# The second routing pass of the first expert network: eight short pieces before the gating of rows 8 to 15, instead of four after the gating of rows 9 to 12

## The reference, cut to what matters

```
def _route(x, gate_weight, expert_bias):
    logits = x @ gate_weight.T                  # 16 experts
    scores = jax.nn.sigmoid(logits)
    biased = scores + expert_bias[None, :]
    ... # the best 2 of 4 groups of 4, by the sum of their two best
    ... # the best 4 experts of the groups kept
    w = jnp.take_along_axis(scores, sel, axis=1)
    w = w / (w.sum(-1, keepdims=True) + 1e-20)
    return (w * SCALING, sel)

def _moe(x, w, sel, gate_proj, up_proj, down_proj):
    cw = (jax.nn.one_hot(sel, NUM_EXPERTS, dtype=x.dtype) * w[..., None]).sum(1)
    def body(acc, inp):
        g, u, d, we = inp
        y = jax.nn.silu(x @ g.T) * (x @ u.T) @ d.T
        return (acc + we[:, None] * y, None)
    out, _ = jax.lax.scan(body, jnp.zeros_like(x), (gate_proj, up_proj, down_proj, cw.T))
    return out
```

## Time and profile before

| | us |
|---|---|
| median of 3 executions | 863.99 |
| lowest, highest | 859.19, 864.0 |
| the profiled execution's own time | 862.82 |
| its span in the profile | 861.1 |
| PE busy | 827.2 (96%) |
| DVE busy | 640.4 (74%) |
| ACT busy | 525.1 (61%) |
| POOL busy | 455.5 (53%) |
| mean granted clock of TensorE | 0.992 |

### The profile page before, as it was taken

The page is one execution under the profiler, slowest core; times in us unless marked ns, Lnnn a source line. Parts: engine busy times, 40 slices in busy tenths (PEclk is TensorE's granted clock), DMA queues, the critical chain, the costliest instruction groups (busy, mean ns, idle before and its releaser), DMA issues.

```text
span 861.1 us, 14804 instructions
## 1 busy us (share of the span) xinstructions
PE 827.2 (96%) x4544; PEld 625.0 (73%) x4544; DVE 640.4 (74%) x1358; ACT 525.1 (61%) x1106; POOL 455.5 (53%) x391
## 2 busy tenths in 40 slices
PE   8899999999999999989999999999999989999997
PEld 6678788878888888767877887754444447888886
DVE  6898788898988888998396866757788644676553
ACT  4778788878888888674544433335566664444442
POOL 3555555555555555732667766531310526656774
PEclk9999999999999999999999999979999999999999
DMA  4232233333222232213765457311441122334451
GB/s 158 93 98 89 97 97 97 100 124 115 94 93 90 95 97 98 80 50 93 224 193 172 131 178 273 105 57 57 147 142 51 57 99 93 123 126 141 151 163 64
DMA packets 57442, 99.20 MB, mean 115 GB/s; under 512 B 8288, under 2 KB 19040, under 8 KB 57376
## 3 DMA queue, kind: packets, MB, share of 16 engines
q1 hardware_dynamic: 57376, 98.39, 35.3%
HBM read 71.88 MB, written 9.57 MB: 95 GB/s over the span
## 4 chain that ended last, share of the span: by engine, by line
PE 69%; DVE 9%; issue 8%; POOL 7%; ACT 3%; DMA 3%; SPq 1%; DVEq 0%; POOLq 0%; ACTq 0%
PE ps L998 10%; PE ps L984 10%; PE ps L975 9%; PE ps L321 7%; PE ps L387 6%; PE ps L335 5%; PE ps L348 4%; PE ps L375 3%; PE ps L1666 3%; PE ps L362 3%; PE ps L1547 2%; PE ps L1636 2%; POOL q_sin L542 2%; DVE nm L1858 2%; PE ps L1570 1%
## 5 line engine op out<-in xcount | busy, mean ns | idle before, releaser
L1122 POOL TENSOR_TENSOR ew_lo<-ew_raw,ew_hi 128x768 fp32r<-128x768 f32 x68 | 128.1, 1885 | 56.5 <-ACT ew_hi L1088 48.5
L1074 ACT ACTIVATE hid_hi<-guw 128x512 fp32r<-128x512 f32 x68 | 43.0, 632 | 156.5 <-POOL guw L1138 106.5
L1177 DVE TENSOR_TENSOR hid_lo<-guw,hid_hi 128x512 fp32r<-128x512 f32 x68 | 80.7, 1186 | 72.1 <-ACT hid_hi L1074 72.0
L1138 POOL TENSOR_TENSOR guw<-gu,cwb 128x512 f32<-128x512 f32 x61 | 80.4, 1319 | 91.0 <-issue 73.9
L542 POOL TENSOR_TENSOR q_sin<-q_sw,sin 128x512 f32<-128x512 f32 x62 | 81.5, 1323 | 73.9 <-DMA q_sw<-q_in 73.0
L1858 DVE TENSOR_REDUCE nm<-ps 128x1 f32<-128x512 f32 x128 | 81.5, 682 | 24.0 <-PE ps L1570 22.8
L1753 ACT ACTIVATE e<-ps 128x512 f32<-128x512 f32 x128 | 68.8, 602 | 40.2 <-PE ps L1666 40.0
L998 PE MATMUL ps<-ew_hi,hid_hi 128*128 128x256 f32 x272 | 78.3, 288 | 2.4 <-DVE hid_lo L1177 1.8
L438 ACT ACTIVATE ex<-sabs,nmax 128x512 f32<-128x512 f32 (+3 forms) x128 | 61.5, 553 | 29.7 <-DVE nmax L502 29.7
L998 PE MATMUL ps<-ew_lo,hid_hi 128*128 128x256 f32 x272 | 76.8, 282 | 0.0
L998 PE MATMUL ps<-ew_hi,hid_lo 128*128 128x256 f32 x272 | 76.8, 282 | 0.0
(11 more groups left out here) (190 smaller groups left out, 2434.1 us busy)
## 6 DMA issues: line engine op xcount, KB each, us to landing
ew_raw<-in_ew SPq DMA_DIRECT2D x68, 384.0 KB, 3.3
q_sw<-q_in SPq DMA_DIRECT2D x128, 128.0 KB, 2.0
cwb<-cw_dram SPq DMA_DIRECT2D x61, 256.0 KB, 3.6
wqk_raw<-in_wqk SPq DMA_DIRECT2D x32, 256.0 KB, 2.7
wv_raw<-in_wv SPq DMA_DIRECT2D x32, 128.0 KB, 2.3
wo_raw<-in_wo SPq DMA_DIRECT2D x32, 128.0 KB, 2.2
qs<-stk_q SPq DMA_DIRECT2D x16, 256.0 KB, 3.6
ks<-stk_k SPq DMA_DIRECT2D x16, 256.0 KB, 4.2
```

The lines of the kernel that those rows point to most:

```text
L1122: pool.tensor_tensor(ff[f].ew[1][:, i % EW_SLOTS, :], ew_raw[:, i % RAW_SLOTS, :], fp(ff[f].ew[0][:, i % EW_SLOTS, :]), ALU.subtract).then ...
L1138: pool.tensor_tensor(ff[f].guw[:, i % 2, :], ff[f].gu[:, i % 2, :], ff[f].cwb[:, r % CWB_SLOTS, :], ALU.mult).then_inc(sem("guw"), 1)
L1177: dve.tensor_tensor(ff[f].hid[1][:, i % 2, :], ff[f].guw[:, i % 2, :], fp(ff[f].hid[0][:, i % 2, :]), ALU.subtract).then_inc(sem("hid_lo"), 1)
```

## The change

Batch 1's routing of the first mixture is cut into eight pieces by four more yields. A piece now stands ahead of `gated(i)` in rows 8 to 15 (behind `hid_low(i-1)` from row 10 on), where four pieces stood at the end of rows 9 to 12. `cw_turn`, `cw_take` and `cw_store` of batch 1 move from row 14 to row 15, on PE, ACT and SP. The instructions themselves are the same. Batch 0's routing and the second mixture keep their pieces and places.

```
-        T1_AT, LOGIT_AT, ROUTE_AT, CW1_AT = ((4, 10), (5, 11), (9, 12), (14, 16))
+        T1_AT, LOGIT_AT, ROUTE_AT, CW1_AT = ((4, 10), (5, 11), (8, 12), (15, 16))
-        ROUTE_PARTS = (4, 3)
+        ROUTE_PARTS = (8, 3)
@@ row_dve
             if i > LAG3:
                 hid_low(dve, f, i - 1)
+            if f == 0 and ROUTE_AT[0] <= i < ROUTE_AT[0] + ROUTE_PARTS[0]:
+                next(route)
             gated(dve, f, i)
@@
-            if ROUTE_AT[f] <= i < ROUTE_AT[f] + ROUTE_PARTS[f]:
+            if f == 1 and ROUTE_AT[1] <= i < ROUTE_AT[1] + ROUTE_PARTS[1]:
                 next(route)
@@ ffn_route, after the sum biased
+                if (f, h) == (0, 1):
+                    yield
@@ after ranked(...) of the groups
+                    if h == 1:
+                        yield
```

## The result

The changed kernel takes 867.58 us (median of 22 executions) where the kernel before took 861.38 in the same comparison. The ratio of the means, without two slow executions of the kernel before (870.56 and 872.31), is 1.0064, with a 95% interval of 1.0043 to 1.0085: 5.5 us slower, between 3.7 and 7.3. The forecast was 865.5, 2.7 above the execution it was worked out on. The sign is right, the time lies in the range, and half of the loss was not in the sum. Part of the nearness of 865.5 to 867.58 is luck: the sum was put on an execution of 862.82, and put on the 861.38 of this comparison it gives 864.1, 3.5 short.

The account below looks back on a forecast made before the run. PE bounds the kernel nearly everywhere, but from row 10 a closed loop of gu, POOL, ACT and hid_lo sets 4.38 us. Pieces 1.2 plus turn 1.5 make 2.7 on 862.82: 865.5, 8-in-10 range 861.0 to 869.5.

Parts of the forecast that it names:

- Pieces 1 and 2: Rows 8 and 9: the pieces meet POOL's low weights; gu(8) 0.5 us late, gu(9) 0.8, gu(10) 0.5, bounds 0 to 1.3.
- Pieces 3 to 8 in the loop at undisturbed price: gu(10) to gu(15): each row takes the loop's 4.38 or 4.68 us plus its whole piece; 27.2 in all, gu(15) 1.2 late.
- Rival A: Rows of the change: gu waits for up on PE in every row, so short pieces are free; 859.6 us; chance 0.13.
- The wait for cw: Turn of cw behind up(15): PE waits 3.7 us for piece 8, which adds 1.5 us, bounds 0 and 3.7.
- 14.7 from gu(15) to the end of down(16): PE's turn, four downs and three gate-up pairs behind gu(15) take 14.7 us, against 13.2 before: 1.5 more.
- Rival B: Turn of cw: only the pieces count, PE's wait for cw is absorbed; 864.0 us; chance 0.15.
- rival C: PE's clock falls to half at the wait in row 15; 6 us more, 871.5, or 868.5 if half as long; chance 0.14.
- the two signs of being wrong: The prediction is wrong if gu(15) starts before 462 us, or if the time changes by more than 5 us.

## Why the prediction was right, and where it was half as large as the loss

**Pieces 1 and 2: right in kind, 0.3 too small.** gu(8) was 0.49 late on the ruler (0.5 was said), gu(9) 1.08 (0.8), gu(10) 0.85 (0.5, within 0 to 1.3).

**Pieces 3 to 8 in the loop at undisturbed price: right.** Said were periods of 5.18, 5.64, 5.41, 5.71 and 5.28; measured 5.18, 5.67, 5.39, 5.60 and 5.12. gu(15) is 1.26 late (1.2), closer than the two terms in it: gu(10) came 0.35 later than said and the five rows took 0.26 less, so a part of that is luck. The last piece cost 0.15 less than said, in part since gu (463.60) starts while the piece's last instruction ends (463.69). Rival A fell with the first of these rows. The timeline of rows 14 and 15 shows what the idea of filling gaps overlooked: DVE has idle time there, but in a place where its next work waits for hid_hi, and the piece was put behind that wait.

**The wait for cw: right.** 3.7 us were said, 3.50 came. 14.7 from gu(15) to the end of down(16) were said; with the wait mostly filled and the clock full it is 14.91, so 1.7 against 1.5. Rival B, that the wait is absorbed, fell with it.

**The clock: the term that was missing.** The sum had nothing for it; I gave rival C 0.14 and priced it at 3 to 6, from the 12 us of the earlier trace rows. It fell in both profiles of the change, and it was short: 3.4 us at half clock, 1.46 on the ruler, half of the lower price. The reasoning for a low chance was that waits of 1.3 us had done no harm. That said nothing of 3.7. The rule cited from the Trainium skill (TensorE: Matmul & The Clock Gate, "HAM oscillation — how this bites in real kernels") spoke for the fall, and the trace of the change agrees, with 0.50 granted once, behind the wait of 3.50. A chance of 0.14 was too low.

In all the ruler moved by 1.28 + 1.72 + 1.46 = 4.46, where 2.7 was said; without the clock it is 3.0. The whole time moved by 5.5 (3.7 to 7.3), which holds 4.46. Whether the remaining 1.0 is anything was not settled: the stages behind the mixture vary by more than that from one execution to the next. Of the two signs of being wrong that the prediction named, gu(15) before 462 did not come (463.60). A change by more than 5 us did by the 5.5, though its interval holds 5 as well; what took it there is the clock, which the sum left out.

The ruler is read from one trace of each kernel. The whole times can be asked as well, since every execution of the experiments has its mean granted clock on record: a straight line through time against clock, with an offset between the two kernels, over the 45 to 47 executions of a comparison. By this estimate 0.01 of mean clock is worth 7 to 8 us. At equal clock the change with the turn in row 16 is 1.0 us slower than the kernel before (0.8 to either side), the change with 13 matmuls 2.9 slower (0.7), the eight pieces behind the gating from row 7 on 1.4 faster (0.7), the kernel without routing 4.4 faster (0.8), and the four pieces from row 6 on 0.1 faster (0.7). The ruler says 1.28 and 3.00 slower, 1.20 and 4.57 faster, and 0.50 slower, which the last interval still holds.

## What to carry to other kernels

Idle time of an engine is room for more work only if the work is put ahead of the wait that makes the idle time; behind it, the whole piece is added to the loop. Even ahead of it the work must not be held there by another engine, as the four long pieces in rows 6 to 9 were. When work is spread over more rows, look at who consumes its last result: here the consumer, one row away in a queue that runs ahead, cost more than the spreading itself. A wait of TensorE has two prices, its own and that of the clock it may lose, and a ruler between two landmarks in the trace repeated within 0.02 us (86.54 and 86.52) where the two executions differed by 11.

## What the runs showed of the hardware that was not expected

- In these rows waits of TensorE of 0.59, 1.52 and 1.71 us left the clock at 1.00, and waits of 1.86 (in the run where POOL waits for hid_lo), 2.05, 2.61 and 3.50 were followed by about 3.4 us at 0.50. Each is one profile, 3.50 two. The length of the wait alone does not decide it. Near 370 us, ahead of the rows of the change, waits of 2.04 and 2.18 were followed by half clock (8 matmuls; eight pieces behind the gating from row 8 on), while waits of 2.06 (the change from row 7 on), 2.15 (the second profile of the change), 2.17 (POOL waits for hid_lo) and 2.18 (4 matmuls) were not. Timeline of PE and stretch from the second profile of the change:

```profile
370.40 0.67 PE L335 MATMUL ps<-q_rot 128*128 128x256 f32 x2 [2.15 <-DVE v L463]
```
```profile
370.00:374.00 4.00, 3.33 (x23) 2.75 (x24) 3.97 (x10) 2.91 (x10) 1.15 (x2) 1.00 0.07 23
```

- POOL's fp32 operation held not only DVE's two-input instructions but also a tensor_scalar with one input in SBUF: 1.81 instead of 0.17. The Trainium skill (SBUF — State Buffer, "Who interferes with whom") counts tensor_scalar among the operations that can take the shared ports, and the row agrees. The first of the two tensor_scalars, at 439.27, had started before POOL and took its 0.17.
- Where a chain of small dependent instructions runs beside POOL, one is held per POOL operation and the rest run free. In the row of gu(14) of the version from row 7 on, the last piece meets two POOL operations and takes 3.4 us, for four instructions that take 0.90 undisturbed: wsume was held for 1.29 and cw for 1.60. Four long pieces in rows 6 to 9 cost 5.08 on the ruler and eight short ones behind the gating from row 7 on 3.37; these two versions differ in rows and in number of pieces at once, so the difference is not put down to either.
